# Second attention of a four-part transformer block: the turned maximum is stored by another queue, one score product moves ahead, and the stage's steps are cut into quarters

## The chip, the cores and the metric

One Trainium2 chip, one of its cores. The metric is the device time of one launch in microseconds; the kernel before took 1277.75 us (median of 3 runs, 1274.56 to 1278.75).

## The reference

The input x has 8 x 512 = 4096 rows of 512 numbers; ctx has 8 x 120 rows of 512. Four layers follow each other, each with a residual:

```
x = x + attention0(layernorm(x), ctx)      # one head
x = x + int8_matmul(layernorm(x), rhs)
x = x + attention1(layernorm(x), ctx)      # 16 heads of 32, output projection w_o
x = x + moe(layernorm(x))                  # 8 routed experts, 1 shared expert

def attention1(query, kv, w_q, w_k, w_v, w_o):
    q, k, v = query @ w_q.T, kv @ w_k.T, kv @ w_v.T         # split into 16 heads
    attn = softmax(einsum("bqhd,bkhd->bhqk", q, k) * 32 ** -0.5)
    return einsum("bhqk,bkhd->bqhd", attn, v) @ w_o.T
```

## The kernel before, in words

The rows are worked in 32 tiles of 128 (NT = 32, four to a batch row). `front` does the first two layers tile by tile, `attention1` the third, `shared` and `experts` the fourth. Matrices are split into a high and a low float16 part, so most products are three matmul passes, and most results leave PSUM twice: ScalarE writes the high part, VectorE or GpSimd the low part as the difference.

`attention1` is a pipeline. In step t every engine runs its `step(t)`, a fixed list of calls for tiles t+6 down to t-5. The heads of a tile go in four groups c = 0 to 3. For tile t the chain is:

- TensorE `scores(t, c)` (L1494): scores of 4 heads into one PSUM bank, used again by the next group.
- VectorE `maximum(t, c)` (L1270): the negative row maximum of each head. `scores(t, c + 1)` waits for it.
- VectorE `shifts(t)`: the 16 maxima of a row as a high part (L1277, a `tensor_scalar`) and a low part (L1279, a `scalar_tensor_tensor`).
- TensorE `shift_transposed(t)` (L1501) turns them; ScalarE `shift_copied(t)` (L1413) brings them out of PSUM; SyncE sends them with two transfers (L1204) into two extra rows of the queries, so that the second score product already holds the subtracted maximum.
- In step t+1 TensorE `scores_transposed(t, c)` (L1518) makes the scores again, keys on the partitions. It waits for these transfers. ScalarE takes two exponentials of them: `exps` (L1398, float32) and `prob_high` (L1407, float16). The low part, their difference, is made by GpSimd for c = 0 and 1 (`prob_low`, L1228) and by VectorE for c = 2 and 3 (`last_low`, L1284). TensorE `outputs(t, c)` (L1534 to L1536) multiplies them with the values.

The queries of a tile go through DRAM: SyncE stores them (L1190), then loads them packed by head (`packed_queries`, L133), and `scores(t, 0)` waits for that. SyncE works through its list in order: store of the queries, rows of tile t-4 (L1194), packed load, the two transfers of the turned maximum, the transposed tile t-4 (L1208), and every fourth step x rows (L1215).

GpSimd also makes the shared expert's weights ready during this stage: `weights(t)` for t = 4 to 27 is one `tensor_tensor` of 128x1024 per step, right after the two `prob_low`. They come in threes: L1239 (which waits for a load), L1242, L1245. The changed VectorE line reads `g.one`, a column of ones (128x1), read over and over.

On TensorE a step is: scores 0, rows_transposed, scores_transposed 0, product 0, scores 1, product 1, scores_transposed 1, product 2, scores 2, product 3, output_transposed, scores_transposed 2, outputs 0, queries 0, scores 3, queries 1, scores_transposed 3, outputs 1, gate_logits, shift_transposed, queries 2, gate_transposed, outputs 2, queries 3, outputs 3.

`stages` weaves the parts together. A step of `attention1` is a generator cut by `yield` into two parts; the table `JOIN` says for each engine and each (step, part) behind which half step of `front` it is issued, and `TAIL` behind which half steps of `attention1` the first pieces of `shared` are.

Of the kernel before, what the change touches and what calls it, by code (L numbers as in the profile page):

```python
# [25 lines left out]
ALU = mybir.AluOpType  # L26
# [3 lines left out]
P = 128  # L30
# [21 lines left out]
COPIES = 3  # L52
# [1057 lines left out]
def attention1(g, io, m, sem, banks, f):  # L1110
# [57 lines left out]
    def sync(sp):  # L1168
        sp.wait_ge(f.j_mm, f.jobs)
        sp.dma_start(gwf[:, :, :], io["gwT"].rearrange("(k p) n -> p k n", p=P)).then_inc(gw_in, 16)  # L1170
        def step(t):
            if live(t) and t % TB == 3:
                b = t // TB
                if b + 1 < B:
                    need(sp, c4["t_mm"], KC * TB * b)
                    if b == 0:
                        sp.wait_ge(f.a["exp"], NT)
                        sp.wait_ge(f.q["y_ok"], NT)
                    packed_keys(sp, g, io, b + 1)
            if 4 <= t < 4 + 3 * B and t % 3 == 1:  # L1180
                b = (t - 4) // 3
                need(sp, w_part, 3 * b)
                if b == 0:
                    sp.wait_ge(f.q["y_mm"], NT)
                sp.dma_start(raw[:, :], io["sh_guT"][b * P:(b + 1) * P, :]).then_inc(w_in, 16)
            u = t + 1
            if live(u):
                sp.wait_ge(s["q_hi"], u + 1)
                sp.wait_ge(s["q_lo"], u + 1)
                sp.dma_start(io["q_rows"][u], qT[:, :, :, :].rearrange("p q k n -> p q (k n)")).then_inc(q_out[u % 2], 16)  # L1190
            v = t - 4
            if live(v):
                sp.wait_ge(lg.ok, v + 1)
                sp.dma_start(io["xn_rows"][v * P:(v + 1) * P, :], lg.xn[:, v % 2]).then_inc(rows_out[v % 2], 16)  # L1194
            if live(u):
                sp.wait_ge(q_out[u % 2], 16 * (u // 2 + 1))
                need(sp, c4["t_mm"], KC * (u - 2))
                if u == 0:
                    sp.wait_ge(f.a["sim"], NT)
                packed_queries(sp, g, io, u, q_in)  # L1200
            if live(t):
                sp.wait_ge(s["n_ok"], t + 1)
                for q in range(2):
                    sp.dma_start(g.queries[t % 3][COPIES * DH + q:COPIES * DH + q + 1].rearrange("p r (c n) -> p (r c) n", n=P),  # L1204
                                 shiftT[q * HEADS:(q + 1) * HEADS, :]).then_inc(n_in, 16)
            if live(v):
                sp.wait_ge(s["g_lo"], v + 1)
                sp.dma_start(io["xt_tiles"][v, :, :], gT[:, v % 2].rearrange("p q k n -> p (q k n)")).then_inc(gt_out[v % 2], 16)  # L1208

            if t >= TB and t % TB == 0:  # L1210
                b = t // TB - 2
                if b >= 0:
                    sp.wait_ge(s["x_new"], TB * (b + 1))
                    rows = io["x_rows"][b * S:(b + 1) * S, :].rearrange("(i p) n -> p i n", p=P)
                    sp.dma_start(rows, g.x[:, b * TB:(b + 1) * TB, :]).then_inc(g.x_out.handle, 16)  # L1215

        def finish():
            for n in range(2):
                sp.wait_ge(rows_out[n], 8 * NT)
                sp.wait_ge(gt_out[n], 8 * NT)  # L1220
        return step, finish

    def gpsimd(pool):
# [23 lines left out]
        def step(t):  # L1247
            if live(t - 4):
                lg.inverse_root(pool, g, t - 4, t % 4)
            if live(t + 4):  # L1250
                ln.inverse_root(pool, g, t + 4, t % 4)
            yield
            prob_low(t - 1, 0)
            prob_low(t - 1, 1)
            weights(t)
        return step, None

    def vector(dve):
# [13 lines left out]
        def shifts(u):  # L1272
            if live(u):
                dve.wait_ge(c4["max"], KC * u + KC)
                need(dve, s["n_mm"], u - 1)
                high, low = (shift[:, q].rearrange("p r c -> p c r") for q in range(2))
                dve.tensor_scalar(high, nmax[:, :], 1 / NS, None, ALU.mult).then_inc(s["shift"], 1)  # L1277
                dve.wait_ge(s["shift"], 2 * u + 1)
                dve.scalar_tensor_tensor(low, nmax[:, :], 1 / NS, high, ALU.mult, ALU.subtract).then_inc(s["shift"], 1)  # L1279

# [80 lines left out]
        def step(t):  # L1361
            if t in (-1, 2):
                key_ones(0 if t < 0 else 1)
            maximum(t, 0)
            query_low(t + 1)
            rows_low(t + 2)
            maximum(t, 1)
            weighted(t - 2)
            yield
            maximum(t, 2)  # L1370
            residual(t - 3)
            gate_stats(t - 3)
            output_low(t - 2)
            maximum(t, 3)
            shifts(t)
            aggregate(lg, t - 3)
            last_low(t - 1, 2)
            stats(ln, t + 6)
            first_rows(t + 3)
            logits(t - 5)  # L1380
            last_low(t - 1, 3)
            aggregate(ln, t + 6)
            gate_low(t - 4)
            if t == 2:
                need(dve, gw_hi, 1)
                dve.scalar_tensor_tensor(gws[:, :, 1], gwf[:, :, :], WS, gws[:, :, 0], ALU.mult,
                                         ALU.subtract).then_inc(gw_lo.handle, 1)
        return step, None

    def scalar(act):  # L1390
# [18 lines left out]
        def shift_copied(u):  # L1409
            if live(u):  # L1410
                act.wait_ge(s["n_mm"], u + 1)
                need(act, n_in, 32 * u)
                act.activation(shiftT[0:2 * HEADS, :], ps_n, ACT.Copy).then_inc(s["n_ok"], 1)  # L1413

        def query_high(u):
            if live(u):
# [36 lines left out]
        def step(t):  # L1453
            query_high(t + 1)
            rows_high(t + 2)
            exps(t - 1, 0)
            prob_high(t - 1, 0)
            gate_rows(t - 4)
            exps(t - 1, 1)
            prob_high(t - 1, 1)  # L1460
# [2 lines left out]
            output_high(t - 2)  # L1463
            exps(t - 1, 2)
            prob_high(t - 1, 2)
            exps(t - 1, 3)
            shift_copied(t)
            prob_high(t - 1, 3)
            gate_high(t - 4)
            if t == NT - 6:  # L1470
# [9 lines left out]
    def tensor(pe):  # L1480
# [131 lines left out]
        def step(t):  # L1612
            scores(t, 0)
            rows_transposed(t + 2)
            scores_transposed(t - 1, 0)
            product(t - 3, 0)
            scores(t, 1)
            product(t - 3, 1)
            scores_transposed(t - 1, 1)
# [3 lines left out]
            product(t - 3, 3)  # L1623
            output_transposed(t - 2)
            scores_transposed(t - 1, 2)
            outputs(t - 1, 0)
            queries(t + 2, 0)
            scores(t, 3)
            queries(t + 2, 1)
            scores_transposed(t - 1, 3)  # L1630
            outputs(t - 1, 1)
            gate_logits(t - 5)
            shift_transposed(t)
            queries(t + 2, 2)
            gate_transposed(t - 4)
            outputs(t - 1, 2)
# [667 lines left out]
def experts(g, io, sem, banks, f):  # L2304
# [209 lines left out]
    def tensor(pe):  # L2514
# [63 lines left out]
    return sync, gpsimd, scalar, vector, tensor  # L2578


JOIN = {
    "sync": {(-6, 0): 62},
    "gpsimd": {(-6, 0): 45, (-6, 1): 47, (-5, 0): 49, (-5, 1): 49, (-4, 0): 51, (-4, 1): 51, (-3, 0): 53, (-3, 1): 53, (-2, 0): 57, (-2, 1): 57, (-1, 0): 61, (-1, 1): 61, (0, 0): 65, (0, 1): 67, (1, 0): 71, (1, 1): 72, (2, 0): 72, (2, 1): 75, (3, 0): 78, (3, 1): 80, (4, 0): 80},
    "scalar": {(-6, 0): 49, (-6, 1): 49, (-5, 0): 49, (-5, 1): 49, (-4, 0): 49, (-4, 1): 49, (-3, 0): 51, (-3, 1): 51, (-2, 0): 59, (-2, 1): 61, (-1, 0): 61, (-1, 1): 63, (0, 0): 65, (0, 1): 69, (1, 0): 71, (1, 1): 76, (2, 0): 76, (2, 1): 78, (3, 0): 80},
    "vector": {(-6, 0): 41, (-6, 1): 41, (-5, 0): 43, (-5, 1): 43, (-4, 0): 45, (-4, 1): 45, (-3, 0): 55, (-3, 1): 58, (-2, 0): 60, (-2, 1): 61, (-1, 0): 62, (-1, 1): 63, (0, 0): 65, (0, 1): 70, (1, 0): 71, (1, 1): 77, (2, 0): 77, (2, 1): 78, (3, 0): 78},
    "tensor": {(-6, 0): 49, (-6, 1): 49, (-5, 0): 49, (-5, 1): 49, (-4, 0): 49, (-4, 1): 49, (-3, 0): 49, (-3, 1): 49, (-2, 0): 59, (-2, 1): 61, (-1, 0): 61, (-1, 1): 63, (0, 0): 65, (0, 1): 70, (1, 0): 71, (1, 1): 77, (2, 0): 77, (2, 1): 79, (3, 0): 79}}


TAIL = {'sync': [67],
        'gpsimd': [],  # L2590
        'scalar': [67, 69, 71, 72],
        'vector': [67, 69, 73],
        'tensor': [63, 65, 67, 67, 70, 71]}


def stages(nc, g, io):


    with ExitStack() as ctx:
# [18 lines left out]
        def both(eng, n, join, after):  # L2618
            begin = first.engines[n](eng)
            step, finish = second.engines[n](eng)  # L2620
            behind = [(s, part) for s in second.steps for part in range(2)]
            running = {}

            def go(steps, s, part):
# [12 lines left out]
            places = list(after)  # L2637
            for s, part in behind:
                go(step, s, part)
                if finish and s == NT + 4 and part == 1:  # L2640
                    finish()
                while places and places[0] <= 2 * s + part:
                    next(last)
                    places.pop(0)
            for tick in last:
# [149 lines left out]
```

## Time and profile before

| | us |
|---|---|
| median of 3 runs | 1277.75 |
| the profiled execution, its own time | 1269.92 |
| span of its trace | 1268.2 |
| TensorE busy | 1183.2 (93%) |
| VectorE busy | 943.8 (74%) |
| ScalarE busy | 650.3 (51%) |
| GpSimd busy | 581.3 (46%) |
| mean granted TensorE clock | 0.983 |

The span runs from the first to the last instruction. `attention1`'s 32 steps start between 232.1 and 587.1 us: step t is counted from the first `scores(t, 0)` matmul to that of the next tile. Engines in the rows: PE is TensorE, DVE VectorE, ACT ScalarE, POOL GpSimd, SP SyncE; a q behind the name is its sequencer. Every tile of this stage lies in one big allocation, so nearly all names in the rows are `att_land`; the line number tells the call.

### The profile page before, as it was taken

The numbers are of one execution on the slowest core, as the hardware profiler recorded it, in microseconds if no ns is written. First come the engines' busy times: TensorE is split into PE (matmuls) and PEld (weight loads), VectorE is DVE, ScalarE is ACT, GpSimd is POOL, SyncE is SP. The second block draws the span as 40 slices with busy tenths as digits, with TensorE's granted clock in tenths as the row PEclk, the third lists the DMA queues.
The fourth block names the chain that finished last, engine by engine and source line by source line (L and its number), as shares of the span: only waits on it lengthen the run. The fifth ranks groups of instructions, "written<-read, shape, count | busy, mean of one in ns | idle before, by whom it ended". The sixth has DMA issues, their size and how long they took to land.

```text
span 1268.2 us, 28634 instructions
## 1 busy us (share of the span) xinstructions
PE 1183.2 (93%) x10724; PEld 806.4 (64%) x10724; DVE 943.8 (74%) x2080; ACT 650.3 (51%) x1183; POOL 581.3 (46%) x690
## 2 busy tenths in 40 slices
PE   6888998779998999997899999999999999999997
PEld 3555655467787888775444444677777777666663
DVE  5899898778899999886486867777777776645451
ACT  4377778557677777764445232221322222465653
POOL 0057678536566666642110000354545454277744
PEclk9999999889999999998999999999999999999999
DMA  9512023123444545462494041304032503599987
GB/s 346 205 67 68 1 33 45 42 72 119 139 162 153 176 143 176 164 180 77 162 171 102 1 133 34 79 23 101 3 100 35 167 6 94 175 252 245 255 141 99
DMA packets 159608, 150.49 MB, mean 119 GB/s; under 512 B 80592, under 2 KB 113520, under 8 KB 159472
## 3 DMA queue, kind: packets, MB, share of 16 engines
q1 hardware_dynamic: 141632, 126.21, 34.7%
q0 software_dynamic: 13248, 21.15, 8.8%
q10 hardware_dynamic: 4592, 1.32, 0.5%
q8 instruction: 86, 1.41, 0.5%
q14 instruction: 50, 0.41, 0.1%
HBM read 84.93 MB, written 57.19 MB: 112 GB/s over the span
## 4 chain that ended last, share of the span: by engine, by line
PE 62%; DVE 9%; DMA 5%; issue 2%; SPq 1%; ACT 1%; POOL 1%; DVEq 0%; ACTq 0%; POOLq 0%
PE bank L124 24%; PE bank L2220 15%; PE bank L2213 13%; PE bank L1587 4%; DVE att_land L1270 2%; DMA q_rows<-att_land 2%; PE bank L1541 1%; PE bank L1518 1%; PE bank L1494 1%; DMA att_land<-att_land 1%; DVE program_x L1343 1%; DVE att_land L1292 1%; DVE att_land L1277 1%; SPq L133 1%; DVE att_land L1311 1%
## 5 line engine op out<-in xcount | busy, mean ns | idle before, releaser
L1718 POOL DMA_INDIRECT lists<-att_land x128 | 132.9, 1038 | 290.5 <-DVE att_land L1859 166.6
L2213 PE MATMUL bank<-att_land 128*128 128x512 f16 x768 | 176.2, 379 | 0.4 <-issue 0.4
L124 PE MATMUL bank<-program_xs,program_wgu 128*128 128x512 f16 x576 | 128.7, 379 | 0.6 <-DVE att_land L1818 0.6
L2213 PEld LDWEIGHTS bank<-att_land 128*128 128x128 f16 x768 | 74.9, 98 | 82.1 <-issue 0.5
L2041 ACT ACTIVATE att_land<-program_x 128x512 f32<-128x512 f32 x40 | 25.2, 631 | 195.1 <-DVE program_x L2183 195.1
L1228 POOL TENSOR_TENSOR att_land<-att_land 120x512 f16<-120x512 f32 x64 | 74.2, 1160 | 109.4 <-ACT att_land L1407 109.4
L124 PE MATMUL bank<-att_land 128*128 128x128 f16 (+1 forms) x1560 | 114.1, 225 | 1.5 <-DVE att_land L1333 1.5
L1587 PE MATMUL bank<-att_land 128*128 128x512 f16 x384 | 107.4, 393 | 0.0
L1270 DVE TENSOR_REDUCE att_land<-bank 128x4 f32<-128x480 f32 x128 | 83.5, 652 | 31.5 <-PE bank L1494 30.7
L1398 ACT ACTIVATE att_land<-bank 120x512 f32<-120x512 f32 x128 | 76.4, 597 | 46.2 <-PE bank L1518 46.2
L124 PEld LDWEIGHTS bank<-program_xs,program_wgu 128*128 128x128 f16 x576 | 56.0, 98 | 67.6 <-DVE att_land L1818 1.1
L124 PEld LDWEIGHTS bank<-att_land 128*128 128x128 f16 x1560 | 92.7, 99 | 6.1 <-DVE att_land L1333 1.7
L2382 POOL DMA_INDIRECT out_rows<-program_x,att_land x40 | 69.7, 1743 | 34.6 <-ACT program_x L2423 19.5
L2220 PE MATMUL bank<-program_x 128*128 128x256 f16 x720 | 85.2, 273 | 0.0
L124 PE MATMUL bank<-program_x 128*128 128x256 f16 (+2 forms) x504 | 80.5, 319 | 0.6 <-DVE program_x L2475 0.6
L1992 ACT ACTIVATE att_land<-att_land 128x512 f16<-128x512 f32 x64 | 40.3, 629 | 71.5 <-PE bank L2213 30.4
L1407 ACT ACTIVATE att_land<-bank 120x512 f16<-120x512 f32 x128 | 76.4, 597 | 0.0
L2220 PEld LDWEIGHTS bank<-program_x 128*128 128x128 f16 x720 | 70.4, 98 | 8.2
L451 POOL TENSOR_TENSOR program_x<-program_x,att_land 128x512 f32<-128x512 f32 x32 | 40.9, 1279 | 75.2 <-ACT att_land L569 75.2
L124 PE MATMUL bank<-program_wgu,att_land 128*128 128x120 f16 (+1 forms) x480 | 52.3, 252 | 17.3 <-DVE att_land L770 14.6
L2052 DVE TENSOR_TENSOR att_land<-att_land 128x512 f16<-128x512 f32 x64 | 44.0, 688 | 31.9 <-ACT att_land L1992 31.8
L124 PEld LDWEIGHTS bank<-program_x 128*128 128x128 f16 x504 | 49.2, 98 | 29.0 <-DVE program_x L2475 1.1
(320 smaller groups left out, 3001.2 us busy)
## 6 DMA issues: line engine op xcount, KB each, us to landing
xn_rows<-att_land SPq DMA_DIRECT2D x37, 256.0 KB, 2.9
out_rows<-att_land SPq DMA_DIRECT2D x37, 256.0 KB, 2.6
att_land<-q_rows SPq DMA_DIRECT2D x66, 128.0 KB, 2.6
q_rows<-att_land SPq DMA_DIRECT2D x32, 256.0 KB, 2.7
xt_tiles<-att_land SPq DMA_DIRECT2D x32, 256.0 KB, 2.2
x_rows<-program_x SPq DMA_DIRECT2D x8, 1024.0 KB, 5.2
att_land<-x_rows SPq DMA_DIRECT2D x8, 1024.0 KB, 5.6
program_xs<-xt_tiles SPq DMA_DIRECT2D x28, 256.0 KB, 5.5
```

What stands on the lines that cost most here:

```text
L124: last = pe.matmul(out, lhs(a, k), rhs(b, k), start=n == 0, stop=n == len(terms) - 1)
L451: pool.tensor_tensor(g.x[:, u, :], g.x[:, u, :], y[:, u % 2], ALU.add).then_inc(a["x_new"], 1)
L1228: pool.tensor_tensor(pT[0:J, c, 1], prob[0:J, c], pT[0:J, c, 0], ALU.subtract).then_inc(c4["p_lo"], 1)
L1270: dve.tensor_reduce(nmax[:, c], ps_s[:, :, :], AX.X, ALU.max, negate=True).then_inc(c4["max"], 1)
L1398: act.activation(prob[0:J, c], ps_t[c % 2][0:J, :], ACT.Exp).then_inc(c4["exp"], 1)
L1407: act.activation(pT[0:J, c, 0], ps_t[c % 2][0:J, :], ACT.Exp).then_inc(c4["p_hi"], 1)
L1587: last = pe.matmul(ps_y[:, :], oT[:, u % 2, a, k, :], g.wo1[:, b, k, :], start=k == 0 and n == 0, stop=k == KC - 1 and n == 2)
L1718: pool.indirect_dma_start(out=io["lists"], out_offset=bass.IndirectOffsetOnAxis(ap=index[:, t, k:k + 1], axis=0), in_=load[:, t, k, :], in ...
L2052: tt(hid[:, v % 2, 1], hf[:, v % 2], hid[:, v % 2, 0], ALU.subtract).then_inc(s["h_lo"].handle, 1)
L2213: last = pe.matmul(ps_y[i][:, :], hid[:, c % 2, a, i * P:(i + 1) * P], wd[:, q, c, :], start=c == 0 and n == 0, stop=c == NC - 1 and n == 2)
L2220: last = pe.matmul(out, lhs(a, k), rhs(q, k), start=n == 0, stop=n == len(terms) - 1)
L2382: pool.indirect_dma_start(out=io["out"], out_offset=bass.IndirectOffsetOnAxis(ap=lst[:, u * CT + n, 0:1], axis=0), in_=res[:, c, n, :], in ...
```

## The change

Five edits, all in `attention1` and in the tables that place it.

1. The two transfers of the turned maximum are issued by ScalarE (new function `shift_rows`, between `exps(t-1, 3)` and `prob_high(t-1, 3)`) and no longer by SyncE. `shift_copied(t)` moves ahead of `exps(t-1, 3)`.
2. TensorE: `scores(t, 3)` comes ahead of `outputs(t-1, 0)` and `queries(t+2, 0)`; `shift_transposed(t)` comes ahead of `scores_transposed(t-1, 3)`, `outputs(t-1, 1)` and `gate_logits(t-5)`.
3. VectorE: `maximum(t, 3)` and `shifts(t)` come ahead of `output_low(t-2)` and of `gate_stats(t-3)`; within the last part `last_low(t-1, 2)`, `logits` and the statistics change places.
4. The high part of the shift is a `scalar_tensor_tensor` (times 1/NS, times `g.one`) in place of the `tensor_scalar`.
5. A step has four parts in place of two, `JOIN` and `TAIL` are rewritten in quarters.

```diff
 # SyncE, step
-            if live(t):
-                sp.wait_ge(s["n_ok"], t + 1)
-                for q in range(2):
-                    sp.dma_start(g.queries[t % 3][...], shiftT[q * HEADS:(q + 1) * HEADS, :]).then_inc(n_in, 16)
 # GpSimd, step
             prob_low(t - 1, 0)
+            yield
             prob_low(t - 1, 1)
+            yield
             weights(t)
 # VectorE, shifts
-                dve.tensor_scalar(high, nmax[:, :], 1 / NS, None, ALU.mult).then_inc(s["shift"], 1)
+                dve.scalar_tensor_tensor(high, nmax[:, :], 1 / NS, g.one[:, 0:1].rearrange("p (o n) -> p o n", o=1)
+                                         .to_broadcast([P, KC, HC]), ALU.mult, ALU.mult).then_inc(s["shift"], 1)
 # VectorE, step
             maximum(t, 2)
             residual(t - 3)
-            gate_stats(t - 3)
-            output_low(t - 2)
             maximum(t, 3)
             shifts(t)
+            output_low(t - 2)
+            yield
+            gate_stats(t - 3)
+            last_low(t - 1, 2)
+            logits(t - 5)
+            stats(ln, t + 6)
             aggregate(lg, t - 3)
-            last_low(t - 1, 2)
-            stats(ln, t + 6)
             first_rows(t + 3)
-            logits(t - 5)
             last_low(t - 1, 3)
 # ScalarE, new, and step
+        def shift_rows(u):
+            if live(u):
+                act.wait_ge(s["n_ok"], u + 1)
+                for q in range(2):
+                    act.dma_start(g.queries[u % 3][...], shiftT[q * HEADS:(q + 1) * HEADS, :]).then_inc(n_in, 16)
             prob_high(t - 1, 2)
+            shift_copied(t)
+            yield
             exps(t - 1, 3)
-            shift_copied(t)
+            shift_rows(t)
             prob_high(t - 1, 3)
 # TensorE, step
             scores_transposed(t - 1, 2)
+            scores(t, 3)
             outputs(t - 1, 0)
             queries(t + 2, 0)
-            scores(t, 3)
             queries(t + 2, 1)
+            shift_transposed(t)
+            yield
             scores_transposed(t - 1, 3)
             outputs(t - 1, 1)
             gate_logits(t - 5)
-            shift_transposed(t)
             queries(t + 2, 2)
 # tables
-TAIL = {'sync': [67], 'gpsimd': [], 'scalar': [67, 69, 71, 72], 'vector': [67, 69, 73],
-        'tensor': [63, 65, 67, 67, 70, 71]}
+TAIL = {"sync": [131], "gpsimd": [], "scalar": [135, 137, 142, 143], "vector": [135, 139, 150],
+        "tensor": [126, 130, 134, 139, 143, 147]}
```

The old `TAIL` counts half steps (2t + part), the new one quarter steps (4t + part). In `JOIN` the parts of the steps from -3 on keep their places up to three half steps of `front` on every engine.

## Rows read from the trace of the kernel before

**Rows 1.** The page: its first two lines, span and busy time of each engine.
```profile
span 1268.2 us, 28634 instructions
PE 1183.2 (93%) x10724; PEld 806.4 (64%) x10724; DVE 943.8 (74%) x2080; ACT 650.3 (51%) x1183; POOL 581.3 (46%) x690
```
**Rows 2.** Windows: length, busy (instructions) per engine; 25 steps, then two single ones.
```profile
279.05:553.95 274.90, 255.65 (x4011) 213.81 (x4008) 246.50 (x543) 200.94 (x374) 170.26 (x221) 0.99 0.49 155
443.31:453.63 10.32, 10.09 (x167) 8.56 (x164) 9.87 (x23) 8.02 (x16) 7.06 (x10) 1.00 0.34 117
464.86:474.94 10.08, 10.08 (x168) 8.55 (x164) 9.62 (x23) 8.02 (x16) 6.87 (x10) 1.00 0.36 121
```
**Rows 3.** Waits of TensorE, 250 to 600: us in total, times, longest.
```profile
PE bank L1501 <- DVE att_land L1279: 6.2, 12, 1.1
PE bank L1494 <- DMA program_xs<-q_rows: 5.7, 3, 2.6
PE bank L1518 <- DMA att_land<-att_land: 4.7, 6, 1.2
...
PE bank L1518 <- DMA program_xs<-att_land: 2.6, 3, 1.2
```
**Rows 4.** Timeline of TensorE in one step: start, duration, line, operands.
```profile
447.87 0.39 PE L1518 MATMUL bank<-program_xs,att_land 98*120 98x128 f16 x4
...
449.07 0.38 PE L1494 MATMUL bank<-att_land 96*128 96x120 f16 x4
...
449.95 0.39 PE L1518 MATMUL bank<-program_xs,att_land 98*120 98x128 f16 x4
...
451.06 0.23 PE L1501 MATMUL bank<-front_id,att_land 128*32 128x128 f16 x1 [0.23 <-DVE att_land L1279]
```
**Rows 5.** Timeline of VectorE in the same step.
```profile
447.64 0.69 DVE L1343 SCALAR_TENSOR_TENSOR program_x<-bank,program_x 128x512 f32<-128x512 f32 x1
...
449.56 0.65 DVE L1270 TENSOR_REDUCE att_land<-bank 128x4 f32<-128x480 f32 x1
450.25 0.53 DVE L1277 TENSOR_SCALAR att_land<-att_land 128x16 f16<-128x16 f32 x1
450.81 0.20 DVE L1279 SCALAR_TENSOR_TENSOR att_land<-att_land 128x16 f16<-128x16 f32 x1
...
452.25 0.68 DVE L1284 TENSOR_TENSOR att_land<-att_land 120x512 f16<-120x512 f32 x1
```
**Rows 6.** Timeline of GpSimd in that step and in the one from 464.86.
```profile
448.60 2.13 POOL L1245 TENSOR_TENSOR program_wgu<-att_land,program_wgu 128x1024 f16<-128x1024 f32 x1
...
470.16 1.89 POOL L1242 TENSOR_TENSOR program_wgu<-att_land,program_one 128x1024 f16<-128x1024 f32 x1
```
**Rows 7.** All 32 instructions of L1277: duration in ns, least, median, most.
```profile
L1277 DVE TENSOR_SCALAR att_land<-att_land x32: 185/294/1445, 249.7 to 597.7; 128x16 f16<-128x16 f32 x32
```
**Rows 8.** Timelines of VectorE and GpSimd where other two-input operations meet GpSimd's.
```profile
396.50 2.23 DVE L1284 TENSOR_TENSOR att_land<-att_land 120x512 f16<-120x512 f32 x1
...
396.29 1.89 POOL L1239 TENSOR_TENSOR att_land<-att_land,program_ws 128x1024 f32<-128x1024 f32 x1 [3.05 <-DMA att_land<-in_sh_guT]
...
81.07 1.21 DVE L643 SCALAR_TENSOR_TENSOR att_land<-program_x,att_land 128x1024 f16<-128x1024 f32 x1
86.92 1.62 DVE L643 SCALAR_TENSOR_TENSOR att_land<-program_x,att_land 128x1024 f16<-128x1024 f32 x1
...
86.19 1.28 POOL L473 TENSOR_TENSOR program_x<-program_x,att_land 128x512 f32<-128x512 f32 x1
```
**Rows 9.** Timelines of SyncE and ScalarE: transfers issued, and ScalarE's last high part.
```profile
451.62 1.15 SPq L1204 DMA_DIRECT2D att_land<-att_land  x2
...
451.50 0.57 ACT L1407 ACTIVATE att_land<-bank 120x512 f16<-120x512 f32 x1
...
539.64 3.85 ACTq L1100 DMA_DIRECT2D program_xs<-xt_tiles  x4
```
**Rows 10.** Waits of TensorE from 597 to 650, where the stage ends.
```profile
PE bank L1607 <- issue: 2.9, 3, 1.8
```

More of the change, by code:

```diff
@@ L1200, in step @@
                 packed_queries(sp, g, io, u, q_in)
-            if live(t):
-                sp.wait_ge(s["n_ok"], t + 1)
-                for q in range(2):
-                    sp.dma_start(g.queries[t % 3][COPIES * DH + q:COPIES * DH + q + 1].rearrange("p r (c n) -> p (r c) n", n=P),
-                                 shiftT[q * HEADS:(q + 1) * HEADS, :]).then_inc(n_in, 16)
             if live(v):
@@ L1413, in shift_copied @@
                 act.activation(shiftT[0:2 * HEADS, :], ps_n, ACT.Copy).then_inc(s["n_ok"], 1)
+        def shift_rows(u):
+            if live(u):
+                act.wait_ge(s["n_ok"], u + 1)
+                for q in range(2):
+                    act.dma_start(g.queries[u % 3][COPIES * DH + q:COPIES * DH + q + 1].rearrange("p r (c n) -> p (r c) n", n=P),
+                                  shiftT[q * HEADS:(q + 1) * HEADS, :]).then_inc(n_in, 16)
         def query_high(u):
@@ L1465, in step @@
             prob_high(t - 1, 2)
+            shift_copied(t)
+            yield
             exps(t - 1, 3)
-            shift_copied(t)
+            shift_rows(t)
             prob_high(t - 1, 3)
@@ L1616, in step @@
             product(t - 3, 0)
+            yield
             scores(t, 1)
@@ L1625, in step @@
             scores_transposed(t - 1, 2)
+            scores(t, 3)
             outputs(t - 1, 0)
             queries(t + 2, 0)
-            scores(t, 3)
             queries(t + 2, 1)
+            shift_transposed(t)
+            yield
             scores_transposed(t - 1, 3)
@@ L2578, in experts @@
     return sync, gpsimd, scalar, vector, tensor
[L2581 to L2586, printed above, removed]
@@ L2589 @@
[L2589 to L2592, printed above, removed]
-        'tensor': [63, 65, 67, 67, 70, 71]}
+JOIN = {"sync": {(-6, 0): 60, (-6, 1): 68},
+    "gpsimd": {(-6, 0): 45, (-6, 1): 45, (-6, 2): 47, (-6, 3): 47, (-5, 0): 49, (-5, 1): 49, (-5, 2): 49, (-5, 3): 49, (-4, 0): 50, (-4, 1): 50, (-4, 2): 53, (-4, 3): 53, (-3, 0): 53, (-3, 1): 53, (-3, 2): 53, (-3, 3): 53, (-2, 0): 54, (-2, 1): 54, (-2, 2): 57, (-2, 3): 57, (-1, 0): 61, (-1, 1): 61, (-1, 2): 61, (-1, 3): 61, (0, 0): 65, (0, 1): 65, (0, 2): 67, (0, 3): 67, (1, 0): 71, (1, 1): 72, (1, 2): 73, (1, 3): 73, (2, 0): 73, (2, 1): 73, (2, 2): 73, (2, 3): 73, (3, 0): 78, (3, 1): 78, (3, 2): 80, (3, 3): 80, (4, 0): 80, (4, 1): 83},
+    "scalar": {(-6, 0): 49, (-6, 1): 49, (-6, 2): 49, (-6, 3): 52, (-5, 0): 52, (-5, 1): 52, (-5, 2): 52, (-5, 3): 52, (-4, 0): 52, (-4, 1): 52, (-4, 2): 52, (-4, 3): 52, (-3, 0): 52, (-3, 1): 52, (-3, 2): 52, (-3, 3): 52, (-2, 0): 59, (-2, 1): 59, (-2, 2): 61, (-2, 3): 61, (-1, 0): 61, (-1, 1): 61, (-1, 2): 63, (-1, 3): 63, (0, 0): 65, (0, 1): 65, (0, 2): 69, (0, 3): 69, (1, 0): 70, (1, 1): 70, (1, 2): 76, (1, 3): 76, (2, 0): 76, (2, 1): 76, (2, 2): 78, (2, 3): 78, (3, 0): 80, (3, 1): 81},
+    "vector": {(-6, 0): 39, (-6, 1): 39, (-6, 2): 39, (-6, 3): 41, (-5, 0): 43, (-5, 1): 43, (-5, 2): 45, (-5, 3): 45, (-4, 0): 45, (-4, 1): 45, (-4, 2): 45, (-4, 3): 46, (-3, 0): 55, (-3, 1): 55, (-3, 2): 57, (-3, 3): 58, (-2, 0): 60, (-2, 1): 60, (-2, 2): 61, (-2, 3): 61, (-1, 0): 62, (-1, 1): 62, (-1, 2): 62, (-1, 3): 62, (0, 0): 66, (0, 1): 66, (0, 2): 70, (0, 3): 70, (1, 0): 71, (1, 1): 71, (1, 2): 77, (1, 3): 77, (2, 0): 77, (2, 1): 77, (2, 2): 78, (2, 3): 78, (3, 0): 78, (3, 1): 78},
+    "tensor": {(-6, 0): 48, (-6, 1): 48, (-6, 2): 48, (-6, 3): 48, (-5, 0): 48, (-5, 1): 48, (-5, 2): 48, (-5, 3): 48, (-4, 0): 48, (-4, 1): 48, (-4, 2): 48, (-4, 3): 48, (-3, 0): 48, (-3, 1): 48, (-3, 2): 48, (-3, 3): 48, (-2, 0): 61, (-2, 1): 61, (-2, 2): 61, (-2, 3): 61, (-1, 0): 61, (-1, 1): 61, (-1, 2): 63, (-1, 3): 63, (0, 0): 65, (0, 1): 65, (0, 2): 70, (0, 3): 70, (1, 0): 71, (1, 1): 71, (1, 2): 77, (1, 3): 77, (2, 0): 77, (2, 1): 77, (2, 2): 79, (2, 3): 79, (3, 0): 79, (3, 1): 79}}
@@ L2596, in stages @@
+TAIL = {"sync": [131],
+        "gpsimd": [],
+        "scalar": [135, 137, 142, 143],
+        "vector": [135, 139, 150],
+        "tensor": [126, 130, 134, 139, 143, 147]}
 def stages(nc, g, io):
@@ L2620, in both @@
             step, finish = second.engines[n](eng)
-            behind = [(s, part) for s in second.steps for part in range(2)]
+            behind = [(s, part) for s in second.steps for part in range(4)]
             running = {}
@@ L2639, in both @@
                 go(step, s, part)
-                if finish and s == NT + 4 and part == 1:
+                if finish and s == NT + 4 and part == 3:
                     finish()
-                while places and places[0] <= 2 * s + part:
+                while places and places[0] <= 4 * s + part:
                     next(last)
```

## The prediction

> **What bounds the kernel now.** I read the page first: TensorE is busy 93% of the span [rows 1]. The change touches one stage, so the windows came next. Over the 25 steps that start at 279.05 a step takes 274.9 / 25 = 11.0 us; an undisturbed one takes 10.08, and TensorE is busy through all of it; the one from 443.31 takes 10.32 [rows 2]. So TensorE's in-order list sets the step, every stall on it adds to the time, and some 0.9 us per step are stalls. VectorE is close behind with 9.6 us busy in the 10.08.
>
> The waits say which stalls [rows 3]. `shift_transposed` (L1501) waits for VectorE's low shift: 6.2 us, 12 times. `scores_transposed` (L1518) waits for the transfers of the turned maximum: 4.7 + 2.6 = 7.3 us, 9 times. `scores` (L1494) waits for packed queries in five steps, 5.7 us for one buffer alone; nothing here shortens that path. The first two are what the change can take away: 13.5 us.
>
> Then the timelines of one step, start 443.31, all places below counted from it. TensorE: `scores_transposed 2` at +4.56, the old `scores 3` at +5.76, `scores_transposed 3` at +6.64, `shift_transposed` at +7.75 after 0.23 idle [rows 4]. VectorE: residual at +4.33, `maximum 3` at +6.25, high shift at +6.94 for 0.53 us, low shift at +7.50 [rows 5]. GpSimd: the weights operation from +5.29 to 450.73, +7.42 [rows 6]. The high shift ended at 450.78, 0.05 after GpSimd's operation; alone it takes 0.185, at worst 1.445 [rows 7]. It is held until GpSimd is done.
>
> **The order on TensorE and VectorE (edits 2 and 3).** The five calls from `scores_transposed 2` to `queries 1` stay the same set, so `shift_transposed` can now start where `scores_transposed 3` did, +6.64. `scores 3` follows `scores_transposed 2` directly. A step where nothing is late keeps its 10.08 us. On VectorE `maximum 3` follows the residual, but needs `scores 3`. That one started at +5.76 and its maximum at +6.25 behind other work; in the first group of a step the maximum starts 0.41 after its scores. New `scores 3` at 4.56 + 0.23 = +4.79, `maximum 3` at +5.20, the high shift 0.69 later (450.25 - 449.56) at +5.89. Free, high and low are done at +6.3: TensorE waits for nothing.
>
> **The high shift (edit 4).** +5.89 is 0.6 us after the weights operation has begun, in every step that has L1242 or L1245: from prob_low's end at +5.3 to +7.19 or +7.42 [rows 6]. Before, the shift came at +6.94 and met only the tail. So all depends on whether a `scalar_tensor_tensor` is held too. L1279 itself never began under a GpSimd operation and says nothing. Others do [rows 8]: L1284, two SBUF inputs, took 2.23 us in place of 0.68 when it began 1.68 before the end of L1239 (396.29 + 1.89 = 398.18; it ended 0.55 after). And L643, a `scalar_tensor_tensor` of two SBUF inputs, took 1.62 with L473 running its last 0.55 us, 1.21 without. Operations with one input from PSUM (the residual at +4.33, L1333) keep their time. The new high shift reads `nmax` and `g.one`, both in SBUF. I take it as held: end of GpSimd's operation + 0.05. The other end is not held at all; that is the first rival.
>
> The Trainium skill ("SBUF — State Buffer", Who interferes with whom) says the same against the change: a VectorE instruction with two SBUF inputs contends with a GpSimd instruction that reads SBUF, and whoever issues first keeps the shared ports for the whole instruction. If only its other case held (the two-port modes, which `tensor_scalar` can enter and this form cannot), the time would be the first rival's.
>
> Held, high ends at +7.24 (L1242) or +7.47 (L1245), the low part 0.22 later, TensorE starts 0.05 after that: +7.51 or +7.75 in place of +6.64. Behind the wait stand `scores_transposed 3`, `outputs 1` and all the rest of the step, so the step grows by 0.87 or 1.11.
>
> - L1242, 8 steps: 8 x 0.87 = 7.0.
> - L1245, 8 steps, of which the one from 540 us is set by the queries' transfers: 7 x 1.11 = 7.8.
> - L1239, 8 steps: it waits for its load and starts at +6.2 or later, behind the shift, in seven. In one it starts at +5.4: 1.0. In four it now covers `last_low 2` (due at +7.5, held to +8.3, all behind it 0.6 to 0.8 late, of which `outputs 3` has 0.3 in hand): 4 x 0.45 = 1.8. Three are set by the queries' transfers: nothing.
>
> Sum of new waits 17.6.
>
> **What goes.** All of L1501's old waits, -6.2 (the new ones above are counted whole). Of the 7.3 of L1518 those outside the step from 540: -6.3. The copy out of PSUM is earlier by 0.25 in the held steps and by 1.1 in the free ones, and SyncE's other transfers no longer stand ahead of it.
>
> **ScalarE's queue (edit 1).** Two issues took 1.15 us on SyncE, where nobody waited [rows 9]. On ScalarE they stand between `exps 3` and `prob_high 3`. `prob_high 3` started at +8.19, its low part at +8.94 [rows 5, 9], and `outputs 3` is due at +10.0, 0.4 after the low part's end. In the free order: copied by +7.1, issued to +8.35, `prob_high 3` 0.2 later than before. In the held one everything on ScalarE hangs on TensorE's +7.5 and keeps its distance. I take 0: the 0.4 us in hand hide it. `gate_high` behind it waits for `gate_transposed` anyway. A dearer issue is the second rival. The Trainium skill ("DMA: Bandwidth & Descriptors", Issuing engines are not separate DMA queues) holds that another issuing engine saves only issue time, the transfers share the same DMA engines; so a slow landing would stay, which would leave some of the 6.3.
>
> SyncE waits for `g_lo` right after, as before, so its later transfers start no earlier.
>
> **Places and parts (edit 5).** A yield costs nothing; TensorE's list at the joint is the same but for the moves above. At the end three filler products of the next stage move half a step to a step later; the stalls there are three of L1607, 2.9 us [rows 10]. Between -2.9 and +2.9; I take 0, since no row says which side.
>
> **Sum.** 17.6 - 6.2 - 6.3 = +5.1 us. The profiled execution took 1269.92, which makes 1275.0. It lies 7.8 below the median of the runs shown, 1277.75; on that footing 1282.9, so **1283 us**. A measurement of this kernel tells 0.3%, 3.8 us, from no change.
>
> **Rivals.**
> A. The new instruction isn't held: its second input is one column read again, and only the two-port form of `tensor_scalar` suffered. For: the low shift always took 0.195. Against: L643 and L1284. Then nothing is late at +6.64: 1277.75 - 12.5 = 1265. 15 to 20%.
> B. ScalarE pays for the issues. Its four issues at 539.64 took 3.85, 0.96 each [rows 9]. Two at that price are 0.78 longer than 1.15; with 0.2 in hand 0.55 us a step late for `last_low 3` and `outputs 3`, 31 steps: +17, 1300. It decides once two issues take more than 1.4 us. Against: those are large transfers into the same tile from four tiles of DRAM, and the same two issues took 1.15 on the other queue. 7%.
> C. Held, but for no net: the end of the stage and the joint win back up to their 2.9, and the queries' waits absorb some of the new ones (a step set by a transfer doesn't grow). 1283 - 4 = 1279. 25%.
> My forecast 50%, its own range 1277 to 1289.
>
> **Range and chances.** 80%: 1266 to 1289, from just above A to the top of the forecast's range. Faster by over 0.3% (below 1273.9): A and a little of C, 0.20. Slower (above 1281.6): B and four fifths of the forecast, 0.48. Within: 0.32.
>
> **What would show it.** The new line's duration: about 1.35 and 1.6 us in sixteen steps if held, 0.2 in all 32 if not. `shift_transposed` then has gaps of 0.9 and 1.1 behind L1279 in these steps, 14 to 16 us in all, and steps take 10.95 and 11.2. The waits of L1518 on transfers should be near 1 us. ScalarE's two issues should take about 1.2, and `outputs 3` should wait for `last_low 3` in few steps. It is wrong if the high shift begins ahead of GpSimd's operation (then A's time without A's reason), or if the first half of a step gets longer.

## The result, and the profile after

The changed kernel takes 1285.38 us (median of 4 runs, 1285.05 to 1286.72), the one before 1276.67 (4 runs, 1274.56 to 1278.75); ratio 1.0082, 95% interval 1.0055 to 1.0109. It is slower, by 8.7 us by the medians. The forecast was 1283, slower, within 1266 to 1289.

The profiled execution took 1285.18 us, its span is 1283.4 us against 1268.2 [rows 1]. The trace of before is of a quick execution, 6.8 us under its median, so the 15.2 us between the traces overstate the loss against the medians; where they lie is still to be read. The same 25 steps of the stage as in [rows 2], then a step with L1237 (the old L1242), one with L1240 (the old L1245) and one without a weights operation; length, then busy time of each engine:

```profile
280.93:569.50 288.57, 258.14 (x4012) 212.38 (x4008) 264.05 (x543) 199.37 (x373) 162.80 (x221) 1.00 0.46 147
441.70:452.77 11.07, 10.31 (x169) 8.53 (x164) 10.67 (x23) 8.02 (x16) 6.60 (x10) 1.00 0.58 205
486.66:497.95 11.29, 10.31 (x168) 8.53 (x165) 10.89 (x23) 8.02 (x16) 6.82 (x10) 1.00 0.57 200
569.50:579.77 10.27, 10.24 (x168) 8.53 (x164) 8.87 (x21) 7.98 (x16) 3.83 (x5) 1.00 0.35 117
```

The 25 steps take 288.57 us against 274.90, 13.7 of the 15.2; the forecast's sum was 5.1. The two held kinds take 11.07 and 11.29 where 10.95 and 11.19 were worked out. But the step with nothing held takes 10.27, not 10.08: that is a part the forecast had left out.

The waits of TensorE from 250 to 610 in the changed kernel, to stand beside [rows 3] (us in total, times, longest). L1511 is `shift_transposed`, L1504 `scores`, L1544 `outputs`, L1528 `scores_transposed`:

```profile
PE bank L1511 <- DVE att_land L1277: 17.3, 21, 1.1
PE bank L1504 <- DVE att_land L1267: 7.4, 5, 3.0
PE bank L1544 <- DVE att_land L1282: 7.3, 11, 1.1
PE bank L1504 <- DMA program_xs<-q_rows: 4.5, 3, 2.1
PE bank L1504 <- DMA att_land<-q_rows: 2.1, 1, 2.1
...
PE bank L1528 <- DMA att_land<-att_land: 0.9, 2, 0.5
```

The waits for the transfers fell from 7.3 to 0.9 as meant. Those for the shift rose from 6.2 to 17.3. `outputs` now waits for `last_low` 7.3 us, which nothing in [rows 3] shows at that size (the same view of before has 2.7 there). Of the 7.4 on L1267, the maximum, one of 3.0 follows ScalarE's four large issues at the end of step 26; the kernel before has these issues too, with a wait of 1.2 behind them. The rest of the 7.4 is at the joint with `front`.

The held step from 441.70: VectorE, GpSimd and TensorE in the changed kernel (start, duration), to stand beside [rows 4 to 6]:

```profile
446.90 0.66 DVE L1267 TENSOR_REDUCE att_land<-bank 128x4 f32<-128x480 f32 x1 [0.18 <-PE bank L1504]
447.60 1.35 DVE L1274 SCALAR_TENSOR_TENSOR att_land<-att_land,program_one 128x16 f16<-128x16 f32 x1
448.98 0.20 DVE L1277 SCALAR_TENSOR_TENSOR att_land<-att_land 128x16 f16<-128x16 f32 x1
```
```profile
447.00 1.90 POOL L1237 TENSOR_TENSOR program_wgu<-att_land,program_one 128x1024 f16<-128x1024 f32 x1
```
```profile
449.23 0.23 PE L1511 MATMUL bank<-front_id,att_land 128*32 128x128 f16 x1 [0.72 <-DVE att_land L1277]
```

The high shift starts 5.90 after the step's start (+5.89 was worked out), 0.60 after GpSimd's operation, and ends at 448.95, 0.05 after GpSimd's 448.90. All 32 of the new instruction (ns, least, median, most); in the kernel before the median was 294 [rows 7]:

```profile
L1274 DVE SCALAR_TENSOR_TENSOR att_land<-att_land,program_one x32: 195/1344/1771, 249.7 to 610.1; 128x16 f16<-128x16 f32 x32
```

ScalarE in that step:

```profile
449.50 0.27 ACT L1413 ACTIVATE att_land<-bank 32x128 f16<-32x128 f32 x1 [1.45 <-PE bank L1511]
449.86 0.60 ACT L1398 ACTIVATE att_land<-bank 120x512 f32<-120x512 f32 x1
449.87 1.16 ACTq L1419 DMA_DIRECT2D program_xs<-att_land  x2
451.07 0.60 ACT L1407 ACTIVATE att_land<-bank 120x512 f16<-120x512 f32 x1 [0.62 <-issue]
```

The last high part waits 0.62 us for its own queue, which is issuing the two transfers.

One more thing differs between the two kernels, and the forecast has no term for it: the clock that TensorE was granted. The mean over a run is 0.984 to 0.986 in the four runs of the changed kernel and 0.973 to 0.983 (mean 0.979) in the 46 runs of the kernel before that stand beside the experiments; the traced one has 0.983. Among those 46 the time follows the clock, for instance from 1271.42 us at 0.982 to 1279.61 at 0.976: by a straight line fitted to each group of runs, each us more of span x (1 - clock) goes with 0.8 us more of time. As an estimate from these numbers, 1280 x 0.006 x 0.8, the higher clock gives 6 us back to the changed kernel; its stalls would then cost some 15 us, as between the traces, and not 8.7. One stretch at half clock (1.2 of 2.4 GHz) lies in step 0 of the kernel before, while the changed kernel has the full clock in all of step 0 (length, busy time of each engine, then the granted clock, here 0.50 and 1.00):

```profile
235.60:245.80 10.20, 7.39 (x23) 3.04 (x23) 5.02 (x15) 4.26 (x7) 5.35 (x9) 0.50 0.22 66
238.00:252.00 14.00, 9.63 (x101) 6.61 (x102) 11.86 (x31) 7.61 (x13) 9.69 (x18) 1.00 0.16 48
```

A stretch of 10.2 us there is in the traces of all three kernels with the old tables (before, experiments 6 and 7) and in none of the other nine. What in the order of work lowers the clock was not tried.

### The profile page after: what moved, and what is told of

The parts are those of the page before. It is cut to its first block, busy times and chain, and to the rows that moved or that the text cites. A ratio compares the mean times of both kernels' runs of the same rounds, so it can differ in the third digit from the quotient of the medians.

```text
span 1283.4 us, 28618 instructions
## 1 busy us (share of the span) xinstructions
PE 1184.1 (92%) x10708; PEld 805.1 (63%) x10724; DVE 961.1 (75%) x2080; ACT 650.4 (51%) x1183; POOL 574.2 (45%) x690
## 3 DMA queue, kind: packets, MB, share of 16 engines
q10 hardware_dynamic: 6640, 1.58, 0.7%
## 4 chain that ended last, share of the span: by engine, by line
PE 75%; DVE 13%; DMA 4%; issue 3%; ACT 2%; POOL 1%; ACTq 1%; SPq 1%; DVEq 0%; POOLq 0%
PE bank L124 25%; PE bank L2232 14%; PE bank L2225 13%; PE bank L1597 6%; PE bank L980 3%; PE bank L1551 2%; DVE att_land L1274 2%; PE bank L1528 2%; DMA q_rows<-att_land 2%; PE bank L1504 2%; DVE att_land L1267 2%; PE bank L1049 1%; PE bank L897 1%; PE bank L1544 1%; DVE front_amax L793 1%
## 5 line engine op out<-in xcount | busy, mean ns | idle before, releaser
L124 PE MATMUL bank<-att_land 128*128 128x128 f16 (+1 forms) x1560 | 107.8, 224 | 3.0 <-DVE att_land L1331 3.0
L1267 DVE TENSOR_REDUCE att_land<-bank 128x4 f32<-128x480 f32 x128 | 83.5, 652 | 23.8 <-PE bank L1504 21.2
```

What stands on the lines that cost most here:

```text
L124: last = pe.matmul(out, lhs(a, k), rhs(b, k), start=n == 0, stop=n == len(terms) - 1)
L1267: dve.tensor_reduce(nmax[:, c], ps_s[:, :, :], AX.X, ALU.max, negate=True).then_inc(c4["max"], 1)
```

## The experiments

Theory H: the high shift is held while GpSimd's weights operation runs. Theory Q: ScalarE's queue pays for the two issues. Theory P: the rewritten places at the joint and the end cost the time. Ratios are to the kernel before on the same chip.

**1. Two of three weights operations early** (GpSimd idles at that place).

```diff
             yield
+            if (t - 4) % 3 != 0:
+                weights(t)
             prob_low(t - 1, 0)
             yield
             prob_low(t - 1, 1)
             yield
-            weights(t)
+            if (t - 4) % 3 == 0:
+                weights(t)
```

> The changed kernel, but on GpSimd the second and third weights operation of each three are issued ahead of prob_low 0 (about +0.6 of a step, GpSimd idle there) and no longer after prob_low 1; the first, which waits for its load, stays. Theory H (the high shift is held by GpSimd's weights operation, both read SBUF): the high shift takes 0.2 us in these 16 steps, the gap before shift_transposed goes, their length falls from 11.07 and 11.29 to about 10.3; 16 x 0.9 = 14 us less than the changed kernel's 1285.4: 1271, and faster than the kernel before. Theory Q (the cost is ScalarE's two issues per step): no change, 1285. Theory P (the joint's and the end's places): no change, 1285.

Measured: 1273.34 us, ratio 0.9996 (0.9974 to 1.0017). In that kernel L1277 is the high shift and L1514 `shift_transposed`:

```profile
L1277 DVE SCALAR_TENSOR_TENSOR att_land<-att_land,program_one x32: 194/196/1841, 246.5 to 597.1; 128x16 f16<-128x16 f32 x32
```

Its waits of TensorE over the stage (us in total, times, longest):

```profile
PE bank L1547 <- DVE att_land L1285: 9.5, 13, 1.4
PE bank L1507 <- DVE att_land L1270: 5.8, 5, 1.6
PE bank L1514 <- DVE att_land L1280: 5.3, 6, 1.2
```

The median falls from 1344 to 196 ns, the waits for the shift from 17.3 to 5.3, the held steps to 10.27. Neither the queue nor the places were touched, so neither Q nor P alone is the cause, and the granted clock is that of the changed kernel, 0.985 in the mean. The long holds that remain in the steps, 1.2 us at most of waiting, are with the first operation of a three, which stayed. But it is not faster than before: `outputs` still waits 9.5 us for `last_low` (L1547 on L1285).

**2. The old form in the new place.**

```diff
-                dve.scalar_tensor_tensor(high, nmax[:, :], 1 / NS, g.one[...].to_broadcast([P, KC, HC]), ALU.mult, ALU.mult)
+                dve.tensor_scalar(high, nmax[:, :], 1 / NS, None, ALU.mult)
```

> The changed kernel with the high shift as the tensor_scalar of before (edit 4 undone, all else kept). Theory H: the form does not matter, it is held until the weights operation ends in the same steps; 1285, within 2 us. If the new form were what costs (or what helps), the time would move: 1277 if the tensor_scalar in this place is not held, 1290 and more if it is held in more steps or longer.

Measured: 1287.32 us, 1.0093 (1.0061 to 1.0125); the waits for the shift are 18.3 us, 23 times, and

```profile
L1274 DVE TENSOR_SCALAR att_land<-att_land x32: 184/1141/1767, 248.9 to 609.5; 128x16 f16<-128x16 f32 x32
```

Edit 4 does nothing measurable: both forms are held.

**3. The transfers on SyncE again**, as in the code of before; `shift_copied` keeps its new place.

> The changed kernel with the two transfers of the turned maximum issued by SyncE again, in the place of before (edit 1's queue undone; ScalarE still copies ahead of exps 3). Theory Q: the whole loss of 8.7 us comes back, 1277. Theory H: only the last 0.1 to 0.2 us of a step come back (an undisturbed step 10.27 to 10.08, a held one 11.07 to 10.95), 32 x 0.13 = 4: 1281; the gaps before shift_transposed stay at 0.72 and 0.95; the waits of scores_transposed on the transfers may rise by up to 3 us.

Measured: 1280.43 us, 1.0034 (1.0007 to 1.006). The gaps before `shift_transposed` are 0.72 and 0.95 as ever (15.5 us in 20), undisturbed steps take 10.06, held ones 10.96 and 11.19, as H says. Waits on this kernel's transfers of the maximum come back at 2.4 us, `outputs` waits 2.1 for `last_low` instead of 7.3. In us it lies between the two expected values, nearer to H's 1281; its ratio, 1.0034, is the one that 1281 would give on the first measurement's footing. So ScalarE's issues have a part in the loss, 0.48%, and the hold has the larger one.

**4. The order of before, all else of the change kept.** `scores 3`, `maximum 3`, `shifts` and `shift_transposed` in their old places, `shift_copied` and `shift_rows` behind `exps 3`, and VectorE's last part in its old order.

> The changed kernel with the order of TensorE, VectorE and ScalarE as before (scores 3, maximum 3, shifts and shift_transposed in their old places), keeping ScalarE's queue, the new form and the new tables. Theory H: the high shift starts at +6.94 again and is held for 0.3 to 0.5 us only; steps of 10.1 to 10.4; the waits of scores_transposed on the transfers mostly stay; 1277 to 1280. Theory Q: the issues still cost, 1285.

Measured: 1287.5 us, 1.0096 (1.006 to 1.0132). H's number is missed, Q's is near. The waits:

```profile
PE bank L1544 <- DVE att_land L1282: 25.2, 30, 2.0
...
PE bank L1511 <- DVE att_land L1277: 3.8, 10, 1.2
```

The long holds are gone (3.8 us of waiting are left, less than the 6.2 of the kernel before), and `outputs` waits for `last_low` 30 times, once in nearly every step, 0.72 in each quiet one. With the late copy of before, the two issues have no slack at all in front of `prob_high 3`. The new order is what makes room for ScalarE's queue, and it is what walks into GpSimd's operation.

**5. Experiments 1 and 3 together.**

> The changed kernel with both: the second and third weights operation of each three ahead of prob_low 0, and the two transfers issued by SyncE as before. What is left of the change is the order, the new form and the tables. Theory H+Q (hold in 16 steps, and 0.1 to 0.2 us a step for ScalarE's issues, adding up): undisturbed steps of 10.06, the waits on the turned maximum's transfers up by 2 to 3 us; 2 to 4 us below the first experiment's 1273.3: 1270, ratio to before about 0.997. Rival (the two costs overlap, one hides the other): 1273.

Measured: 1265.01 us, 0.9912 (0.9881 to 0.9943), more than was expected. Undisturbed steps are 10.06 to 10.12. Taking both away gives 1.70% where each alone gives 0.86% (hold) and 0.48% (queue), 1.34% together. The 0.36% between them isn't clear of the four intervals of some 0.25% each (0.5% when combined), so no more is shown than that the two costs are both there and roughly add up. The expected 2 to 4 us for the queue were too few: from experiment 1 to this one it is 0.84%.

**6. The kernel before with two of three weights operations early**, the same edit as in 1.

> The kernel before, with only the second and third weights operation of each three moved ahead of prob_low 0. Theory H: the high shift of before meets only the last 0.1 to 0.5 us of these operations; L1277 then takes 0.19 us in these steps, seven gaps of 0.23 before shift_transposed go: 2 us, ratio 0.998. The three long holds by the first operation (1.2 to 1.4 us) stay. Rival (the early place delays prob_low 0 and its outputs): slower by 1 to 5 us.

Measured: 1271.06 us, 0.9968 (0.9945 to 0.9992). Its high shift (a `tensor_scalar`) takes 188 ns in the median in place of 294, the waits for the shift are 3.0 us in place of 6.2. The kernel before was touched by the hold too.

**7. Old places.** `JOIN` and `TAIL` of before, written in quarters.

> The changed kernel with JOIN and TAIL of before, written in quarters (each old first part is new parts 0 and 1, each second part 2 and 3; on GpSimd part 0, and 1 to 3). Theory H+Q: the stage's steps 4 to 27 are as in the changed kernel; the start of step 0 (238.0 against 232.1 before) may come back, but step 3 starts only 1.9 later than before, so at most 2 us at the joint and 2 at the end: 1283 to 1287. Theory P: the places cost the loss, 1277.

Measured: 1289.47 us, 1.0094 (1.0066 to 1.0122), not to be told from the changed kernel's 1.0082. So edit 5 doesn't cause the loss; a gain by it of up to some 0.5% lies within the intervals. Its runs have the lower clock of the kernel before, 0.980 in the mean, with the half-clock stretch in step 0.

**8. All weights operations a step later and early; load, packed keys and x rows behind the packed queries.**

```diff
+            weights(t - 1)
             prob_low(t - 1, 0)
 ...
-            weights(t)
 # SyncE, behind packed_queries: packed_keys (a step earlier), the load of sh_guT, the store of x rows
```

> The changed kernel (rows of the maximum on ScalarE), with all three weights operations a step later and ahead of prob_low 0, and on SyncE the load of the weights, the packed keys (one step earlier) and the store of x rows behind the packed queries instead of ahead of the store of the queries. Theory H: no high shift is held in any step, so beyond the first experiment the five steps 4, 10, 16, 19, 22 lose 3 to 4 us of gaps and last_low is held nowhere: 3 us more. Theory D (the queries' waits in steps 8, 14, 26, 30, 8 us in all, come from the 0.5 and 1 MB transfers issued ahead of the store of the queries): they fall below 3 us. Together 1273.3 - 3.5 - 3 - 5 = 1262, ratio 0.990. If the waits come from something else: 1267.

Measured: 1276.58 us, 0.9989 (0.9966 to 1.0012): a miss: 0.990 was expected, so by 0.9%, 11 us. Theory D was right on its own wait: those for the packed queries, 4.5 and 2.1 us, are down to one of 1.3 in the whole stage. But the waits for the turned maximum rose from 0.9 to 11.0:

```profile
PE bank L1548 <- DVE att_land L1286: 10.6, 13, 2.3
PE bank L1532 <- DMA att_land<-att_land: 8.7, 8, 2.0
...
PE bank L1532 <- DMA program_xs<-att_land: 2.3, 3, 0.9
```

The large transfers had only been moved from one short transfer's way into another's.

**9. Experiment 1 with the issues behind `prob_high 3`.**

```diff
             exps(t - 1, 3)
-            shift_rows(t)
             prob_high(t - 1, 3)
+            shift_rows(t)
```

> The first experiment's kernel (second and third weights operations early, rows of the maximum on ScalarE) with shift_rows issued behind prob_high 3 instead of ahead of it. Theory Q (what ScalarE's queue costs is the delay of prob_high 3, and with it of last_low 3 and outputs 3): prob_high 3 starts at about +7.9 and not +8.6, undisturbed steps are 10.06 and not 10.27, the waits of outputs on last_low fall from 8.4 to about 2 us; ratio to before 0.991, as with SyncE issuing (1265). Rival (any issue on ScalarE costs, by gate_high or by the later transfers): ratio 0.996 to 1.000, as in the first experiment, with waits on gate_high or on the transfers.

Measured: 1266.17 us, 0.9919 (0.9895 to 0.9942), as Q says. ScalarE in one step of experiment 1, then in the same step here:

```profile
384.50 0.27 ACT L1416 ACTIVATE att_land<-bank 32x128 f16<-32x128 f32 x1 [0.67 <-PE bank L1514]
384.87 0.60 ACT L1401 ACTIVATE att_land<-bank 120x512 f32<-120x512 f32 x1
384.87 1.15 ACTq L1422 DMA_DIRECT2D att_land<-att_land  x2
386.07 0.60 ACT L1410 ACTIVATE att_land<-bank 120x512 f16<-120x512 f32 x1 [0.61 <-issue]
```
```profile
379.18 0.27 ACT L1416 ACTIVATE att_land<-bank 32x128 f16<-32x128 f32 x1 [0.67 <-PE bank L1514]
379.55 0.60 ACT L1401 ACTIVATE att_land<-bank 120x512 f32<-120x512 f32 x1
379.56 0.51 ACTq L1422 DMA_DIRECT2D att_land<-att_land  x1
380.04 0.59 ACT L1410 ACTIVATE att_land<-bank 120x512 f16<-120x512 f32 x1
380.10 0.61 ACTq L1422 DMA_DIRECT2D att_land<-att_land  x1
```

From the copy to the last high part it is 1.57 us there and 0.86 here. The waits of `outputs` on `last_low` fall from 9.5 to 4.7 (2 were expected), undisturbed steps are 10.06. Two lines in another order are worth 0.8%, of which a clock of 0.987 in place of 0.985 is a part. With the issues behind the work that others wait for, ScalarE's queue costs nothing that can be measured: the ratio is that of experiment 5, where SyncE issues them.

**10. Experiment 9 with all weights operations early and their load right behind the store of the queries.**

> The previous kernel, with all three weights operations a step later and ahead of prob_low 0, and their load issued right behind the store of the queries (not behind the packed queries). Theory H: no hold in any step; the four long holds and the three late last_low of the previous one go, 5 us; the waits of scores on packed queries stay or fall a little. 1260, ratio 0.987. Rival (as in the last experiment: large loads at this place meet the transfers of the turned maximum, whose waits rise by as much as is won): 1265 or more, waits of scores_transposed on transfers above 5 us.

Measured: 1256.43 us, 0.9842 (0.982 to 0.9864), the fastest of all and 21 us below the kernel before beside it. It also has the highest clock, 0.990 against 0.979; by the 0.8 of above, an estimate, that is half of the 21 us. The high shift and the waits:

```profile
L1274 DVE SCALAR_TENSOR_TENSOR att_land<-att_land,program_one x32: 194/195/1086, 249.5 to 580.7; 128x16 f16<-128x16 f32 x32
```
```profile
PE bank L1504 <- DMA program_xs<-q_rows: 4.1, 4, 1.9
PE bank L1528 <- DMA att_land<-att_land: 3.7, 5, 1.3
...
PE bank L1511 <- DVE att_land L1277: 2.3, 3, 0.9
PE bank L1544 <- DVE att_land L1282: 1.8, 4, 0.7
```

The one hold left is at the joint: the high shift of 1.09 us starts at 261.71, under a `prob_low` of GpSimd from 261.59 to 262.74, and ends 0.06 after it. The three waits on the shift are 0.46 behind this hold and two of 0.9 in the last two steps, where nothing is held. Why the waits on transfers stayed low here and not in experiment 8 is open: the load's place, the places of keys and x rows, and the place of the issues on ScalarE all differ.

## Why the prediction was right, and where it was off

- **The number** was hit in part by luck. The forecast went from trace to trace and then added 7.8 us, the distance of the traced execution from the median in the kernel before. From trace to trace it had +5.1 and 1275.0; measured are +15.3 and 1285.2, 10.2 too few. The changed kernel's own distance from trace to median is 0.2 us, so the added 7.8 were 7.6 too many. The two errors leave the 2.5 us between 1283 and 1285.4. The distance goes with the clock: 0.983 in the trace of before against 0.979 in the mean of its runs beside the experiments, 0.985 in both for the changed kernel.
- **What bounds the stage** (TensorE's in-order list, every stall adds): right; held steps grew by their gaps.
- **The place of the high shift**, +5.89: measured +5.89 to +5.92 in every step where nothing else is late. **Its length** "1.35 and 1.6 in sixteen steps if held": 1.35 and 1.58. **Shown** as the cause by experiment 1; that the form is without effect, by experiment 2. Rival A is out.
- **Sum of new waits 17.6**, of which 15.8 on the shift: measured 17.3 in 21 waits on the shift. The L1237 and L1240 steps with nothing else late were right to 0.1 us or so in length. The step that the working left out as set by the queries' transfers (step 27, from 540.29 in the kernel before) grew too, from 13.66 to 14.82: its hold came on top of the late transfer. The first operations of the threes met the shift in four steps (4, 10, 16, 22), not in one, because they could start earlier, at +5.3 to +5.8; why they did is not settled. For `last_low` 1.8 were taken, in four steps. It was held in three, `last_low 2` in one (2.32 us, in the step from 464.11) and `last_low 3` in two, and `outputs` waited 0.5 to 0.9 behind each; the kernel before had two such holds.
- **What goes, 12.5**: the transfers' waits fell by 6.4, 6.3 was said. That the order alone would give the 12.5 us isn't shown. Experiment 5, nearly free of both costs, is 0.88% (11 us) below the kernel before, but its clock is 0.986 against 0.979, by the 0.8 of above (an estimate) 7 of the 11 us. Its waits for the shift are still 5.8 us (6.2 before), those for the transfers 3.1 (7.3 before), those for packed queries 10.5 (8.0 before), and its steps 4 to 27 take 268.21 us against 265.13, with 10.2 us of them at half clock against 3.4. Experiment 5, then before:

```profile
285.66:553.87 268.21, 249.42 (x3864) 206.96 (x3859) 236.43 (x523) 193.77 (x361) 159.73 (x218) 0.98 0.49 155
288.82:553.95 265.13, 245.96 (x3862) 205.90 (x3859) 237.63 (x523) 194.03 (x361) 166.13 (x215) 0.99 0.49 157
```

- **ScalarE's queue, taken as 0**: this term was mis-sized. Experiment 3 puts it at 0.48%, 6 us, in the changed kernel; experiments 1 and 9 at 0.8%, 10 us, once the hold is gone. The working had `prob_high 3` 0.2 later than before, against +8.19. But +8.19 was read in a step in which the shift was held (the one from 443.31); in the kernel before's free steps `prob_high 3` starts at +7.9. In the changed kernel's free step it starts at +8.6 (with SyncE issuing: +7.9), 0.65 later, more than the 0.4 in hand; `last_low 3` then starts at +9.20 (with SyncE issuing: +8.78 at the latest), and ends after the +9.8 at which `outputs 3` is due. Rival B named this path but tied it to a dearer issue; the issue was as cheap as read (1.16) and the slack smaller.
- **Places, taken as 0**: nothing clear of noise in the time, by experiment 7; the clock differs, as said there.
- **The total**: of the 10.2 us missing between the traces, 8.6 are in the 25 steps. The queue's 6 to 10 us are of that size. Against them stand the 6 us that the higher clock gives back by the estimate above, in the comparison by medians. Finer than that it isn't split.

## What to carry to other kernels

Moving an operation earlier on one engine is also moving it under whatever another engine runs at that time; for a VectorE operation with two SBUF inputs (or a `tensor_scalar` within SBUF), read GpSimd's timeline at the new place first, and move GpSimd's long operation if it can lie where VectorE reads PSUM. A transfer's issue on a compute engine's queue can delay what is listed behind it (here by 0.7 of its 1.15 us), so it goes behind the last instruction that others wait for. Slack is to be read in the kind of step that it will be spent in. Changing the form of a held instruction is worth nothing if the new form is held as well. And before a difference of a few tenths of a per cent is put down to waits, the granted clocks of the two kernels' runs are to be compared.

## What the runs showed of the hardware

- A 128x16 operation of 0.19 us takes 1.35 or 1.58 when it starts 0.6 us into a GpSimd `tensor_tensor` of 1.90 or 2.13, ending 0.05 after it; so for `tensor_scalar` and for `scalar_tensor_tensor` whose second input is one column read again (experiment 2 and the changed kernel). That a broadcast column counts as a second input is consistent with this, but no run tried the same form with a second input outside SBUF. The Trainium skill ("SBUF — State Buffer", Who interferes with whom) has both cases as contending, `tensor_scalar` where its operands allow a two-port mode, and the trace agrees.
- Two issues of 4 KB transfers hold ScalarE's queue for 1.15 us, and an activation listed behind them starts 0.7 us later than one listed ahead (experiments 1 and 9). The Trainium skill ("DMA: Bandwidth & Descriptors", Issuing engines are not separate DMA queues) calls that time usually small beside the transfer; here it was 1.15 for two against a landing of 1.8, on a path with 0.4 us to spare. The transfers landed no sooner for the other queue: medians of 1.8 us from issue on ScalarE, 1.7 and 1.8 on SyncE in the kernel before.
- The mean granted TensorE clock goes with the kernel, not only with the run: 0.973 to 0.983 in 46 runs of the kernel before, 0.984 to 0.986 in 4 of the changed one, 0.988 to 0.991 in 4 of experiment 10; and within the kernel before the time follows it, 0.8 us for each us of span x (1 - clock).
